# A six-stage transformer kernel on one core: the start of masked attention moved into the expert stage, and its scales by logarithm and exponential

## The chip, the cores and the metric

The kernel runs on one core of one Trainium2 chip. The metric is device microseconds of one execution, and the number compared is the median of several runs. Everything is fp32. The engines are TensorE (PE, with PEld for its weight loads), VectorE (DVE), ScalarE (ACT), GpSimd (POOL) and SyncE (SP, which here only issues transfers).

## What is computed

Six layers are applied to 64 batches of 32 rows of 128 numbers, each with a residual. The two that the change touches are the third, a soft mixture of 16 experts, and the fourth, masked cross attention over 257 keys for each batch:

```python
x = x + _L0_ffn_ref(_layernorm(x, axis=-1), ...)       # soft experts
x = x + _L1_xattn_ref(_layernorm(x, axis=-1), ctx_1024, mask_BxS2_bk0, ...)

def _L1_xattn_ref(query, key_value, key_mask, Wq, bq, Wk, bk, Wv, bv, Wo, bo):
    Q = query @ Wq + bq
    K = key_value @ Wk + bk
    V = key_value @ Wv + bv
    scores = jnp.einsum('bqh,bkh->bqk', Q, K) / jnp.sqrt(jnp.float32(hid))
    scores = jnp.where(key_mask[:, None, :], scores, jnp.float32(-1000000000.0))
    attn = jax.nn.softmax(scores, axis=-1)
    context = jnp.einsum('bqk,bkh->bqh', attn, V)
    return context @ Wo + bo
```

## The kernel before

The 2048 rows lie as 16 tiles of 128 rows in `xres`, four batches to a tile. The stages (cross attention, state space, experts, masked attention, causal attention, routed linear) run one after the other. Each is a block of five instruction streams, one for each engine, written out by hand, with semaphores between them. The next block begins on every engine only when all streams of the block before have ended; within a block an engine takes its instructions strictly in the order in which they are written.

**Experts, second part (`expert_layers`).** For each tile t, PE makes the slots' inputs (`gather`, L1828), ACT copies them out of PSUM (`slots_in`, L1880), PE makes the hidden layer (`hidden`, L1835), ACT applies Gelu (L1888), PE makes the second layer (`second`, L1848), DVE adds its bias (`slots_out`, L1907), PE mixes the slots back to rows (`combine`, L1858), and DVE adds the residual (L1912) and makes the row's mean and variance (L2905 to L2910, into `mv`). The PE's order is second(t), hidden(t+1), combine(t), gather(t+2). `gather(t)` waits for the Gelu of tile t-1, since both use a bank, and `second(t)` waits for the residual of tile t-1. GpSimd has no work in this block.

**Masked attention.** It goes in eight pairs of tiles. A pair's front is: rows normalised by DVE (`xn`, L2287), turned by PE (L2032), copied by ACT (L2182); queries by PE (L2037) and ACT (L2188); the queries times the keys' weights by PE (L2042, and a column of biases L2046) and ACT (L2194, `qk_t`), with the biases scaled by DVE (L2295, `qb`). Then the scores against the context (PE, L2056, `s_ps`), the mask (DVE, L2303 and L2311, with `keep` and `drop` made by GpSimd from the byte mask, L2389 and L2392), the exponentials (ACT, L2203), their transposes (PE, L2066, copied by DVE, L2325, `p_t`), the sums over the context (PE, L2089), and the values' and output's weights.

The fronts and scores of pairs 0 and 1 are made ahead; after that `slot(u)` finishes pair u and makes the front of pair u + 2. Before the fronts, the scales of all 16 tiles are made from `mv`: root of the variance on ACT (L83), reciprocal and product on DVE (L90, L92). GpSimd adds the output's bias to all of `xres` at once (L2408, `x_bo`), and DVE's slots wait for that. SP loads two context blocks of pair u + 2 (`room`): the first when pair u's scores are done, the second when its sums are.

Of the kernel before, what the change touches and what calls it, by code (L numbers as in the profile page):

```python
# [8 lines left out]
ALU = mybir.AluOpType  # L9
# [8 lines left out]
QT = 4  # L18
# [53 lines left out]
class NormScales:  # L72
# [1430 lines left out]
def soft_experts(nc, d, weights, xres, ident, mv, rstd, nmr):  # L1503

    C = 2
    with ExitStack() as outer:
# [5 lines left out]
        expert_layers(nc, weights[1], xres, mv, tok.x1, disp, comb_t)  # L1512
# [285 lines left out]
def expert_layers(nc, weights, xres, mv, xn, disp, comb_t):  # L1798
# [5 lines left out]
    with ExitStack() as stack:  # L1804
# [17 lines left out]
        def _(pe):  # L1822
# [29 lines left out]
            def combine(t):  # L1852
# [7 lines left out]
                last.then_inc(out_mm, 1)  # L1860
            pe.wait_ge(w_ld, W_LD)
# [1171 lines left out]
```

## Time and profile before

| | |
|---|---|
| median of three runs | 965.69 us (963.86, 965.69, 965.86) |
| the profiled execution | 960.14 us, of which the profile's span is 958.4 us |
| granted TensorE clock, mean over the span | 0.933 of full speed |
| busy over the span | PE 796.0, PEld 438.8, DVE 726.3, ACT 557.2, GpSimd 208.1 us |
| experts, second part | about 608.6 to 675.9 us |
| masked attention | about 676.9 to 759 us |

Times in the profile are microseconds from the start of its span. Busy shares are averages over six different stages, so they say little about one place; what matters for a change at a boundary of two stages is the order of events there, which the timeline shows. Matmul rows count passes: an fp32 matmul stands as two, a transpose as one.

### The profile page before, as it was taken

What the parts mean: (1) busy time and instruction counts of PE and PEld (TensorE: products, weight loads), DVE (VectorE), ACT (ScalarE), POOL (GpSimd) and SP (SyncE); (2) the same over time, 40 slices, a digit from 0 to 9 for tenths busy, and PEclk for the clock granted to TensorE, in tenths of its full rate; (3) what the DMA queues carried; (4) which work ended last, traced back from release to release, by engine and by line L of the source; (5) the groups of instructions that cost most, each with busy time, mean ns of one, the idle gap of its engine ahead of it and who ended that gap; (6) DMA issues with size and microseconds to landing.
All of it is one profiled execution on the core that took longest, in us unless ns stands there. A gap on an engine that the chain in (4) does not pass through costs nothing. (4 is left out here: it accounts for less than half of the span.)

```text
span 958.4 us, 25493 instructions
## 1 busy us (share of the span) xinstructions
PE 796.0 (83%) x9286; PEld 438.8 (46%) x9286; DVE 726.3 (76%) x2428; ACT 557.2 (58%) x1407; POOL 208.1 (22%) x228
## 2 busy tenths in 40 slices
PE   5899999998866689679757268799699999999876
PEld 2477777776422234224213056466376334343343
DVE  5688888887369999999999778465566486767866
ACT  3698988989674766757525147555244533333445
POOL 1366766766100000000000023000320000000046
PEclk9999999999997799889779599799699999999999
DMA  7111111110000000000000070300175000000001
GB/s 257 30 47 42 38 39 44 38 27 2 2 0 0 0 1 1 0 1 1 0 1 1 1 184 14 166 4 5 45 267 218 1 1 1 1 1 1 1 13 33
DMA packets 23422, 36.67 MB, mean 38 GB/s; under 512 B 5668, under 2 KB 19748, under 8 KB 21156
## 3 DMA queue, kind: packets, MB, share of 16 engines
q1 hardware_dynamic: 23336, 35.53, 11.8%
q8 instruction: 53, 0.87, 0.4%
q14 instruction: 33, 0.27, 0.1%
HBM read 34.48 MB, written 1.05 MB: 37 GB/s over the span
## 5 line engine op out<-in xcount | busy, mean ns | idle before, releaser
L505 ACT ACTIVATE xa_prob<-xa_s,xa_nmax 128x257 f32<-128x257 f32 x256 | 128.1, 503 | 21.1 <-DVE xa_nmax L642 19.3
L789 POOL TENSOR_TENSOR xa_prob<-xa_prob,xa_rinv 128x1028 f32<-128x1028 f32 x64 | 121.5, 1900 | 76.7 <-DVE xa_rinv L649 75.8
L642 DVE CUSTOM_DVE_ANT_0 xa_s<-xa_s_ps,xa_nbias 128x257 f32<-128x257 f32 x256 | 93.2, 420 | 12.3 <-ACT xa_prob L505 6.4
L1784 POOL TENSOR_TENSOR mo_disp_t<-mo_disp_t,mo_rst 128x256 f32<-128x256 f32 x16 | 9.8, 615 | 346.8 <-DVE mo_rst L1745 346.8
L335 PE MATMUL xa_t_ps<-identity,xa_prob 128*128 128x128 f32 x512 | 69.5, 279 | 4.0 <-ACT xa_p_t L514 1.8
L632 DVE COPY xa_kvs<-xa_kv_ps 128x512 f32<-128x512 f32 x64 | 44.1, 689 | 34.3 <-PE xa_kv_ps L309 34.3
L335 PEld LDWEIGHTS xa_t_ps<-identity,xa_prob 128*128 128x128 f32 x512 | 54.8, 141 | 25.6 <-issue 25.6
L514 ACT COPY xa_p_t<-xa_t_ps 128x1024 f32<-128x1024 f32 x64 | 63.4, 991 | 2.2 <-PE xa_t_ps L335 2.2
L948 PE MATMUL ss_bank<-ss_xs,ss_wx 128*128 128x512 f32 x128 | 58.9, 609 | 4.8 <-DVE ss_eps L1402 3.1
L2496 PE MATMUL ca_v_ps<-ca_w_vo,ca_xn_t 128*32 128x512 f32 x512 | 61.2, 596 | 0.5 <-DVE ca_v L2685 0.5
L962 PE MATMUL ss_bank<-ss_xs,ss_wx 128*128 128x512 f32 x128 | 59.9, 624 | 0.0
L2893 POOL TENSOR_TENSOR rl_part<-rl_part 128x256 f32<-128x256 f32 x16 | 11.9, 744 | 188.9 <-ACT rl_part L2841 188.3
L505 ACT ACTIVATION_READ_ACCUMULATOR xa_prob<-xa_s,xa_nmax 128x1 f32 x256 | 48.3, 189 | 0.0
L2489 PE MATMUL ca_z_ps<-ca_xn_t,ca_m_t 128*128 128x512 f32 x96 | 47.6, 618 | 0.7 <-ACT ca_xn_t L2606 0.7
L1131 ACT ACTIVATE ss_sq<-ss_bank 128x512 f32<-128x512 f32 x32 | 19.1, 597 | 49.4 <-PE ss_bank L962 49.4
L324 PE MATMUL xa_s_ps<-xa_kvs,xa_q_blk 32*128 32x257 f32 x512 | 46.2, 430 | 1.9 <-ACT xa_wv_last L485 1.2
L2685 DVE COPY ca_v<-ca_v_ps 128x512 f32<-128x512 f32 x64 | 41.4, 683 | 1.9 <-PE ca_v_ps L2496 1.9
L962 PEld LDWEIGHTS ss_bank<-ss_xs,ss_wx 128*128 128x128 f32 x128 | 25.2, 202 | 37.5 <-issue 37.5
L306 PE MATMUL xa_kv_ps<-xa_ctx_t,xa_wkv 128*32 128x256 f32 x512 | 40.5, 388 | 2.1 <-DMA xa_ctx_t<-in_ctx_t 2.1
L948 PEld LDWEIGHTS ss_bank<-ss_xs,ss_wx 128*128 128x128 f32 x128 | 24.1, 194 | 38.4 <-issue 33.0
L346 PE MATMUL xa_pv_ps<-xa_p_t,xa_kvs 128*32 128x128 f32 x1024 | 41.2, 279 | 0.0
L309 PE MATMUL xa_kv_ps<-xa_wkv,xa_ctx_t 128*32 128x128 f32 x1024 | 40.5, 277 | 0.0
(380 smaller groups left out, 1861.2 us busy)
## 6 DMA issues: line engine op xcount, KB each, us to landing
xa_ctx_t<-in_ctx_t SPq DMA_DIRECT2D x64, 128.5 KB, 2.1
room<-in_ctx_t SPq DMA_DIRECT2D x8, 1028.0 KB, 6.6
room<-in_ctx_n SPq DMA_DIRECT2D x8, 1024.0 KB, 4.9
ss_wx<-in_ss_wx SPq DMA_DIRECT2D x1, 2048.0 KB, 7.9
xres<-in_x SPq DMA_DIRECT2D x4, 256.0 KB, 5.5
out_x<-xres SPq DMA_DIRECT2D x4, 256.0 KB, 2.3
ma_mask_u<-in_mask SPq DMA_DIRECT2D x4, 128.5 KB
room<-in_ca_wk SPq DMA_DIRECT2D x1, 512.0 KB, 3.5
```

Source lines behind the costliest of these rows:

```text
L324: last = nc.tensor.matmul(s_ps[:, g, 0:S], q_blk[rows, r, :, :].rearrange("p h q -> p (h q)"), kvs[rows, r, 0:S], start=True, stop=True)
L335: last = nc.tensor.transpose(t_ps[:, c, g * P:g * P + P], prob[:, r, g, c * P:c * P + P], ident[:, :])
L505: nc.scalar.activation(prob[:, r, g, :], s_sb[:, b, g, :], ACT.Exp, bias=nmax[:, r, g:g + 1], scale=-1.0, accum_out=rsum[:, r, g:g + 1]).t ...
L514: nc.scalar.copy(p_t[:, b % 2, :, :], t_ps[:, :, :]).then_inc(pt_ready, 1)
L632: nc.vector.tensor_copy(kvs[:, r, :].rearrange("p (a s) -> p a s", a=2)[:, :, 0:SP_], kv_ps[:, :].rearrange("p (a s) -> p a s", a=2)).then ...
L642: nc.vector.tensor_tensor_reduce(out=s_sb[:, b, g, :], in0=s_ps[:, g, 0:S], in1=nbias[:, g, :], scale=1.0, scalar=3e38, op0=ALU.add, op1=A ...
L789: nc.gpsimd.tensor_tensor(prob[:, r, :, :], prob[:, r, :, :], bc(rinv[:, r, :].rearrange("p (g o) -> p g o", o=1), (P, G, S)), ALU.mult).t ...
L948: last = nc.tensor.matmul(bank[(2 + i) % 3][:, :], w_x[:, kb, 0, r, h, :], xs[:, c % 3, kb, :], start=(kb == 0), stop=(kb == 1))
L962: last = nc.tensor.matmul(bank[(1 + i) % 3][:, :], w_x[:, kb, 1, r, h, :], xs[:, c % 3, kb, :], start=(kb == 0), stop=(kb == 1))
L2489: nc.tensor.matmul(z_ps[:, n % 2, :], m_t[:, h, :], xn_t[:, QT * q:QT * q + QT, :], start=True, stop=True).then_inc(z_mm, 1)
L2496: last = nc.tensor.matmul(v_ps[N * h:N * h + N, b % 2, :], xn_t[:, t, N * b:N * b + N], w_vo[:, h, :, :], start=True, stop=True)
L2685: nc.vector.tensor_copy(v[:, j, b, :, :].rearrange("p g c -> p (g c)"), v_ps[:, b % 2, :]).then_inc(v_ready, 1)
```

## The change

- The fronts of pairs 0 and 1 (normalised rows, transposes, queries, query keys, bias columns) are made in the experts' block, for tiles 0 to 3, whose residuals have long been final there. DVE's part of normalising goes to GpSimd (`normalise`), DVE's scaling of the bias column to ACT.
- For the scales of tiles 0 to 3, ACT takes a logarithm and an exponential at tile 11, with a load of their table before and of Gelu's after. At the block's end it loads the first table again.
- GpSimd makes the masks of pairs 0 and 1 at the start of the experts' block, and `x_bo` tile by tile, after each residual.
- Masked attention begins with the scores of pairs 0 and 1. Its scales for all tiles are made by logarithm and exponential on ACT (the table is already there); only the product with the mean is left to DVE, after the first pair's masks.
- The tiles for `x_bo`, `keep` and `drop` lie in memory of the causal stage (`ca_xn_t`, `ca_z_first`), and `xn`, `xn_t`, `q_t` and `qk_t` are held twice.

```diff
-        self.root, self.eps = k.sb(f"{st}_norm_root", [P, T]), k.sb(f"{st}_norm_eps", [P, 1])
-        self.eps_set, self.root_ready, self.ready = (k.sem(f"{st}_norm_{n}") for n in ("eps_set", "root_ready", "ready"))
+    def __init__(self, k, st, mv, rstd, nmr, eps):
+        self.nc, self.mv, self.rstd, self.nmr, self.eps = k.nc, mv, rstd, nmr, eps
+        self.log_var = k.sb(f"{st}_norm_log", [P, T])
+        self.log_ready, self.ready = (k.sem(f"{st}_norm_{n}") for n in ("log_ready", "ready"))
 
     def scalar(self, act):
-        act.wait_ge(self.eps_set, 1)
-        self.nc.scalar.activation(self.root[:, :], self.mv[:, :, 1], ACT.Sqrt, bias=self.eps[:, :]).then_inc(self.root_ready, 1)
+        self.nc.scalar.activation(self.log_var[:, :], self.mv[:, :, 1], ACT.Ln, bias=self.eps[:, :]).then_inc(self.log_ready, 1)
+        act.wait_ge(self.log_ready, 1)
+        self.nc.scalar.activation(self.rstd[:, :], self.log_var[:, :], ACT.Exp, scale=-0.5).then_inc(self.ready, 1)
...
+        self.x_bo = sources.xn_t[:, :, :]
+        self.keep, self.drop = (masks[:, n * 4 * S:n * 4 * S + 4 * S].rearrange("p (j i s) -> p j i s", j=2, i=2) for n in range(2))
+        self.xn, self.xn_t, self.q_t = (k.sb("ma_" + n, [P, 2, 2, D]) for n in ("xn", "xn_t", "q_t"))
+        self.qk_t, self.qb = k.sb("ma_qk_t", [P, 2, 2, D]), k.sb("ma_qb", [P, 2, 2])
...
+def masks_of_pair(nc, pool, pairs, mask_u8, u, j, past):
+
+    nc.gpsimd.tensor_copy(pairs.keep[:, j, :, :], mask_u8[:, bass.ds(u * 2, 2), :]).then_inc(pairs.keep_ready, 1)
+    pool.wait_ge(pairs.keep_ready, u + 1)
+    pool.sem_inc(past, 1)
+    nc.gpsimd.tensor_scalar(pairs.drop[:, j, :, :], pairs.keep[:, j, :, :], -1e9, 1e9, ALU.mult, ALU.add).then_inc(pairs.drop_ready, 1)
...
+            def turn_x(u):
+                pe.wait_ge(pairs.xn_ready, u + 1)
+                for i in range(2):
+                    last = nc.tensor.transpose(turn_ps[u][:, i * P:i * P + P], pairs.xn[:, u, i, :], ident[:, :])
+                last.then_inc(pairs.xnt_mm, 1)
+
+            def queries(u):
+                if u == 0:
+                    pe.wait_ge(masked[1], masked[2])
+                pe.wait_ge(pairs.xnt_ready, u + 1)
+                nc.tensor.matmul(q_ps[u], w_q[:, :], pairs.xn_t[:, u, :, :].rearrange("p i c -> p (i c)"), start=True, stop=True).then_inc(pairs.q_mm, 1)
+
+            def query_keys(u):
+                pe.wait_ge(pairs.q_ready, u + 1)
+                nc.tensor.matmul(qk_ps[u], w_kt[:, :], pairs.q_t[:, u, :, :].rearrange("p i c -> p (i c)"), start=True, stop=True)
+                for i in range(2):
+                    last = nc.tensor.matmul(b_ps[u][:, i:i + 1], pairs.q_t[:, u, i, :], b_k[:, :], start=True, stop=True)
+                last.then_inc(pairs.qk_mm, 1)
             pe.wait_ge(w_ld, W_LD)
             gather(0)
             hidden(0)
             gather(1)
             for t in range(T):
                 second(t)
+                if t == T - 1:
+                    queries(1)
+                    query_keys(0)
                 if t + 1 < T:
                     hidden(t + 1)
+                if t == T - 2:
+                    turn_x(0)
+                    turn_x(1)
                 combine(t)
                 if t + 2 < T:
                     gather(t + 2)
+                if t == T - 2:
+                    queries(0)
+            query_keys(1)
...
+            def first_scales():
+                act.wait_ge(pairs.eps_set, 1)
+                act.wait_ge(pairs.mv_ready, QT)
+                nc.scalar.activation(pairs.log_var[:, :], mv[:, 0:QT, 1], ACT.Ln, bias=pairs.eps[:, :]).then_inc(pairs.log_ready, 1)
+                act.wait_ge(pairs.log_ready, 1)
+                nc.scalar.activation(rstd[:, 0:QT], pairs.log_var[:, :], ACT.Exp, scale=-0.5).then_inc(pairs.rstd_ready, 1)
+
+            def xnt(u):
+                act.wait_ge(pairs.xnt_mm, u + 1)
+                nc.scalar.copy(pairs.xn_t[:, u, :, :].rearrange("p i c -> p (i c)"), turn_ps[u]).then_inc(pairs.xnt_ready, 1)
+
+            def queries(u):
+                act.wait_ge(pairs.q_mm, u + 1)
+                nc.scalar.activation(pairs.q_t[:, u, :, :].rearrange("p i c -> p (i c)"), q_ps[u], ACT.Identity, bias=b_q[:, :]).then_inc(pairs.q_ready, 1)
+
+            def query_keys(u):
+                act.wait_ge(pairs.qk_mm, u + 1)
+                nc.scalar.activation(pairs.qk_t[:, u, :, :].rearrange("p i c -> p (i c)"), qk_ps[u], ACT.Identity, scale=NORM).then_inc(pairs.qk_ready, 1)
+                nc.scalar.activation(pairs.qb[:, u, :], b_ps[u], ACT.Identity, scale=NORM).then_inc(pairs.qb_ready, 1)
             nc.scalar.preload_act_table(ACT.Gelu)
             act.wait_ge(w_ld, W_LD)
             slots_in(0)
             hidden(0)
             for t in range(1, T):
+                if t == FIRST - 1:
+                    nc.scalar.preload_act_table_set("natural_log_exp_and_others")
                 slots_in(t)
+                if t == FIRST - 1:
+                    first_scales()
+                    nc.scalar.preload_act_table(ACT.Gelu)
                 hidden(t)
-            nc.scalar.preload_act_table(ACT.Sqrt)
+            xnt(0)
+            xnt(1)
+            nc.scalar.preload_act_table_set("natural_log_exp_and_others")
+            queries(0)
+            queries(1)
+            query_keys(0)
+            query_keys(1)
...
+        @block.gpsimd
+        def _(pool):
+            def normalise(u):
+                if u == 0:
+                    pool.wait_ge(pairs.rstd_ready, 1)
+                for i in range(2):
+                    t = 2 * u + i
+                    last = nc.gpsimd.tensor_scalar(pairs.xn[:, u, i, :], xres[:, t, :], mv[:, t, 0:1], rstd[:, t:t + 1], ALU.subtract, ALU.mult)
+                last.then_inc(pairs.xn_ready, 1)
+            pool.wait_ge(masked[1], masked[2])
+            for u in range(2):
+                masks_of_pair(nc, pool, pairs, mask_u8, u, u, past_p)
+            for t in range(T):
+                if t == FIRST - 1:
+                    normalise(0)
+                if t == FIRST:
+                    normalise(1)
+                pool.wait_ge(res_ready, t + 1)
+                nc.gpsimd.tensor_tensor(pairs.x_bo[:, t, :], xres[:, t, :], b_o[:, :], ALU.add).then_inc(pairs.xbo_ready, 1)
...
             for u in range(2):
-                turn_x(u)
-                queries(u)
-                query_keys(u)
                 scores(u, u)
...
             norm.scalar(act)
-            nc.scalar.preload_act_table_set("natural_log_exp_and_others")
             act.wait_ge(w_ld, W_LD)
-            xnt(0)
-            queries(0)
-            query_keys(0)
-            xnt(1)
-            queries(1)
             exps(0, 0)
-            query_keys(1)
             xnt(2)
             exps(1, 1)
...
+            nc.vector.memset(first.eps[:, :], EPS).then_inc(eps_set, 1)
+            scores(0, 0)
             norm.vector(dve)
-            nc.vector.memset(first.eps[:, :], EPS).then_inc(eps_set, 1)
-            normalise(0)
-            normalise(1)
-            scores(0, 0)
             normalise(2)
             scores(1, 1)
-            dve.wait_ge(xbo_ready, 1)
+            dve.wait_ge(xbo_ready, T)
             steps(dve, slot, 4)
             moments_of(U - 2)
...
-            masks_of(0, 0)
-            masks_of(1, 1)
-            nc.gpsimd.tensor_tensor(x_bo[:, :, :], xres[:, :, :], bc(b_o[:, :].unsqueeze(1), (P, T, D)), ALU.add).then_inc(xbo_ready, 1)
             steps(pool, slot)
```

PE's instructions from the experts' hidden layer of the last tile into the start of masked attention, before (`me_` are the experts' tiles, `ma_` masked attention's, `room` the context; the branches are the ends and beginnings of blocks):

```order
L1835 MATMUL me_in_ps<-me_slot_in,me_w 32x64 x16
L1858 MATMUL me_so_ps<-me_slot_out,mo_comb_t 64x128 x8
L1848 MATMUL me_so_ps<-me_w,me_hid 32x128 x32
L1858 MATMUL me_so_ps<-me_slot_out,mo_comb_t 64x128 x8
L1804 UNCONDITIONAL_BRANCH
L2025 UNCONDITIONAL_BRANCH
L2032 MATMUL ma_f_ps<-identity,ma_xn 128x128 x2
L2037 MATMUL ma_f_ps<-ma_xn_t,ma_w_q 128x256
L2042 MATMUL ma_f_ps<-ma_q_t,ma_w_kt 128x256
L2046 MATMUL ma_b_ps<-ma_b_k,ma_q_t 128x1 x2
L2056 MATMUL ma_s_ps<-room,ma_qk_t 32x257 x8
L2032 MATMUL ma_f_ps<-identity,ma_xn 128x128 x2
```

and of the change, up to the end of the experts' block:

```order
L1863 MATMUL me_in_ps<-me_slot_in,me_w 32x64 x16
L1893 MATMUL me_in_ps<-identity,ma_xn 128x128 x4
L1886 MATMUL me_so_ps<-me_slot_out,mo_comb_t 64x128 x8
L1900 MATMUL me_in_ps<-ma_xn_t,ma_w_q 128x256
L1876 MATMUL me_so_ps<-me_w,me_hid 32x128 x32
L1900 MATMUL me_in_ps<-ma_xn_t,ma_w_q 128x256
L1904 MATMUL me_in_ps<-ma_q_t,ma_w_kt 128x256
L1906 MATMUL me_in_ps<-ma_b_k,ma_q_t 128x1 x2
L1886 MATMUL me_so_ps<-me_slot_out,mo_comb_t 64x128 x8
L1904 MATMUL me_in_ps<-ma_q_t,ma_w_kt 128x256
L1906 MATMUL me_in_ps<-ma_b_k,ma_q_t 128x1 x2
```

Four transposes stand ahead of the next to last mixing, one query matmul ahead of the last second layer, and the other, with one pair's query keys, ahead of the last mixing; the last pair's query keys come behind it. Then masked attention's first rows on PE are:

```order
L2166 MATMUL ma_s_ps<-room,ma_qk_t 32x257 x16
L2142 MATMUL ma_f_ps<-identity,ma_xn 128x128 x2
L2176 MATMUL ma_p_ps<-identity,ma_prob 128x128 x4
L2187 MATMUL ma_l_ps<-identity,ma_p_last 4x128 x2
L2147 MATMUL ma_f_ps<-ma_xn_t,ma_w_q 128x256
L2199 MATMUL ma_c_ps<-room,ma_p_t 32x128 x16
```

The two pairs' scores follow each other (before, a front of four steps stood ahead of each), then the rows of pair 2 are turned.

ACT's instructions around tile 11 of the experts, before (Gelu of tile 10, copies and Gelu of tile 11, and so on):

```order
L1888 ACTIVATE me_hid<-me_in_ps,me_b 128x64 x4
L1880 COPY me_slot_in<-me_in_ps 128x512 x2
L1888 ACTIVATE me_hid<-me_in_ps,me_b 128x64 x4
L1880 COPY me_slot_in<-me_in_ps 128x512 x2
L1888 ACTIVATE me_hid<-me_in_ps,me_b 128x64 x4
```

and of the change:

```order
L1944 ACTIVATE me_hid<-me_in_ps,me_b 128x64 x4
L1972 ACT_TABLE_LOAD
L1936 COPY me_slot_in<-me_in_ps 128x512 x2
L1950 ACTIVATE ma_first_log<-mv,ma_eps 128x4
L1952 ACTIVATE rstd<-ma_first_log 128x4
L1976 ACT_TABLE_LOAD
L1944 ACTIVATE me_hid<-me_in_ps,me_b 128x64 x4
L1936 COPY me_slot_in<-me_in_ps 128x512 x2
```

One table load moved in between Gelu and the copies, and a logarithm, an exponential and another load between the copies and Gelu.

## Rows read from the trace of the kernel before

**Rows 1.** Timeline, experts' last tiles: start us, length us, engine, line, operation, [idle before <-releaser].

```profile
667.29 0.71 PE L1828 MATMUL me_in_ps<-mo_disp,mo_x 32*128 32x256 f32 x8
...
668.07 1.07 ACT L1880 COPY me_slot_in<-me_in_ps 128x512 f32<-128x512 f32 x2 [0.92 <-PE me_in_ps L1828]
...
669.79 1.25 PE L1858 MATMUL me_so_ps<-me_slot_out,mo_comb_t 128*64 128x128 f32 x16
...
669.91 0.93 ACT L1888 ACTIVATE me_hid<-me_in_ps,me_b 128x64 f32<-128x64 f32 x4 [0.77 <-PE me_in_ps L1835]
...
671.53 1.06 PE L1848 MATMUL me_so_ps<-me_w,me_hid 32*32 32x128 f32 x64 [0.48 <-DVE xres L1912]
...
673.37 1.25 PE L1858 MATMUL me_so_ps<-me_slot_out,mo_comb_t 128*64 128x128 f32 x16 [0.79 <-DVE me_slot_out L1907]
...
675.76 0.17 DVE L2910 COPY mv<-me_moments 128x2 f32<-128x2 f32 x1
```

**Rows 2.** Timeline, masked attention's first two pairs.

```profile
676.87 0.61 POOL L2389 CAST ma_keep<-ma_mask_u 128x514 f32<-128x514 uint8 x1 [69.74 <-POOLq L2920]
...
679.67 4.51 POOL L2408 TENSOR_TENSOR ma_x_bo<-xres,ma_b_o 128x2048 f32<-128x2048 f32 x1
...
679.80 4.71 DVE L2287 TENSOR_SCALAR ma_xn<-xres,rstd,nmr 128x128 f32<-128x128 f32 x2 [0.84 <-PE ma_f_ps L2032]
...
684.41 1.94 PE L2056 MATMUL ma_s_ps<-room,ma_qk_t 128*32 128x257 f32 x16 [0.47 <-ACT ma_qk_t L2194]
...
685.78 0.49 DVE L2303 SCALAR_TENSOR_TENSOR ma_s_keep<-ma_s_ps,ma_qb,ma_keep 128x257 f32<-128x257 f32 x1 [1.20 <-PE ma_s_ps L2056]
...
691.55 1.94 PE L2056 MATMUL ma_s_ps<-room,ma_qk_t 128*32 128x257 f32 x16 [0.47 <-ACT ma_qk_t L2194]
...
693.43 0.69 PE L2032 MATMUL ma_f_ps<-identity,ma_xn 128*128 128x128 f32 x2
...
696.18 1.28 PE L2089 MATMUL ma_c_ps<-room,ma_p_t 128*32 128x128 f32 x32
```

**Rows 3.** Windows: length, busy of PE, PEld, DVE, ACT, POOL, PEclk, DMA share, GB/s.

```profile
676.00:678.00 2.00, 0.00 (x0) 0.00 (x0) 0.63 (x5) 0.97 (x2) 0.93 (x2) 0.54 0.00 0
...
691.00:696.00 5.00, 4.53 (x27) 2.52 (x26) 2.58 (x9) 2.10 (x7) 0.91 (x3) 0.50 0.00 0
...
696.00:697.00 1.00, 1.00 (x25) 0.79 (x28) 0.00 (x0) 0.47 (x1) 0.80 (x2) 0.68 0.00 0
```

**Rows 4.** Timeline, ScalarE: a table load and the activation behind it (cross attention).

```profile
21.65 1.28 ACT L588 ACT_TABLE_LOAD   x1
...
22.95 0.51 ACT L505 ACTIVATE xa_prob<-xa_s,xa_nmax 128x257 f32<-128x257 f32 x1
```

**Rows 5.** Timeline, ScalarE: a logarithm of variances in masked attention.

```profile
735.91 0.28 ACT L2227 ACTIVATE ca_log_var<-mv,ca_norm_eps 128x4 f32<-128x4 f32 x1
```

**Rows 6.** Timeline, pairs further on in masked attention.

```profile
698.03 0.70 PE L2042 MATMUL ma_f_ps<-ma_q_t,ma_w_kt 128*128 128x256 f32 x2
...
698.55 0.59 DVE L2287 TENSOR_SCALAR ma_xn<-xres,rstd,nmr 128x128 f32<-128x128 f32 x2
...
698.56 0.50 PE L2046 MATMUL ma_b_ps<-ma_b_k,ma_q_t 128*128 128x1 f32 x4
...
699.54 1.07 PE L2056 MATMUL ma_s_ps<-room,ma_qk_t 128*32 128x257 f32 x16 [0.20 <-ACT ma_qk_t L2194]
...
700.48 0.88 DVE L2303 SCALAR_TENSOR_TENSOR ma_s_keep<-ma_s_ps,ma_qb,ma_keep 128x257 f32<-128x257 f32 x2 [1.22 <-PE ma_s_ps L2056]
...
701.30 0.60 PE L2066 MATMUL ma_p_ps<-identity,ma_prob 128*128 128x128 f32 x4
...
701.97 0.68 DVE L2325 COPY ma_p_t<-ma_p_ps 128x512 f32<-128x512 f32 x1
```

**Rows 7.** Groups of GpSimd's instructions: count | busy us, mean ns | idle before.

```profile
L2895 POOL TENSOR_TENSOR rl_part<-rl_part 128x128 f32<-128x128 f32 x16 | 7.3, 455 | 1.2
```

**Rows 8.** The page's DMA issues: KB each, us from issue to landing.

```profile
room<-in_ctx_t SPq DMA_DIRECT2D x8, 1028.0 KB, 6.6
```

More of the change, by code:

```diff
@@ L1795, in slots, with expert_layers @@
         slot(t, t % 2)
-def expert_layers(nc, weights, xres, mv, xn, disp, comb_t):
+def expert_layers(nc, weights, masked, pairs, xres, ident, mv, rstd, xn, disp, comb_t):
     SL, HID = 16, 32
@@ L1912, in residual @@
                 nc.vector.tensor_tensor(xres[:, t, :], xres[:, t, :], out_ps, ALU.add).then_inc(res_ready, 1)
-                statistics(nc, dve, t, xres, mv, stats, moments, res_ready, st_ready, mo_ready, past_v)
+                last = statistics(nc, dve, t, xres, mv, stats, moments, res_ready, st_ready, mo_ready, past_v)
+                if t < QT:
+                    last.then_inc(pairs.mv_ready, 1)
+            nc.vector.memset(pairs.eps[:, :], EPS).then_inc(pairs.eps_set, 1)
             dve.wait_ge(w_ld, W_LD)
@@ L1965, in masked_attention @@
         ctx_t, ctx_n, ctxt_in, ctxn_in = weights[1]
-        m_t, first = weights[2:]
-        x_bo = k.sb("ma_x_bo", [P, T, D])
-        keep, drop = k.sb("ma_keep", [P, 2, TP, S]), k.sb("ma_drop", [P, 2, TP, S])
-        xn, xn_t, q_t, qk_t = (k.sb("ma_" + n, [P, TP, D]) for n in ("xn", "xn_t", "q_t", "qk_t"))
-        qb, smin, rsum, rinv = (k.sb("ma_" + n, [P, 2, TP]) for n in ("qb", "smin", "rsum", "rinv"))
+        m_t, first, pairs = weights[2:]
+        x_bo, keep, drop = pairs.x_bo, pairs.keep, pairs.drop
+        xn, xn_t, q_t = (a[:, 0, :, :] for a in (pairs.xn, pairs.xn_t, pairs.q_t))
+        qk_t, qb = pairs.qk_t, pairs.qb
+        smin, rsum, rinv = (k.sb("ma_" + n, [P, 2, TP]) for n in ("smin", "rsum", "rinv"))
         s_keep, s_all = k.sb("ma_s_keep", [P, TP, S]), k.sb("ma_s_all", [P, 2, TP, S])
@@ L2385, in masks_of @@
             def masks_of(u, j):
-                if later(u, 1):
-                    pool.wait_ge(sall_ready, TP * (u - 1))
-                    pool.sem_inc(past_p, 1)
-                nc.gpsimd.tensor_copy(keep[:, j, :, :], mask_u8[:, bass.ds(u * TP, TP), :]).then_inc(keep_ready, 1)
-                pool.wait_ge(keep_ready, u + 1)
+                pool.wait_ge(sall_ready, TP * (u - 1))
                 pool.sem_inc(past_p, 1)
-                nc.gpsimd.tensor_scalar(drop[:, j, :, :], keep[:, j, :, :], -1e9, 1e9, ALU.mult, ALU.add).then_inc(drop_ready, 1)
+                masks_of_pair(nc, pool, pairs, mask_u8, u, j, past_p)
             def last_column(u, j):
@@ L2954, in program @@
         ctx = context_room(k, room)
-        run(soft_experts, (mo, me, joining, joined, ctx, tokens))
         sources = FirstSources(k)
-        run(masked_attention, (ma, ctx, joined[0], sources))
+        with ExitStack() as attention:
+            pairs = FirstPairs(Scope(nc, attention), sources)
+            run(soft_experts, (mo, me, joining, joined, ctx, tokens, ma, pairs))
+            run(masked_attention, (ma, ctx, joined[0], sources, pairs))
         routes = FirstRoutes(k, tokens.x1, tokens.mu_u)
```

50 lines of the change are left out of this document (29 added, 21 removed).

## The prediction

> **What bounds the kernel here.** The busy shares of the page say little about a boundary, so I read the timeline of the experts' last tiles first. There PE and ACT pass one tile around a ring. ACT sat idle for 0.92 us before its copies at 668.07, so Gelu had ended at 667.15; the next gather began on PE at 667.29, ACT's copies at 668.07, Gelu at 669.91 after another 0.77 us of waiting, and it ended at 670.84, which is 3.69 us after the Gelu before it [rows 1]. What ACT does in its two waits is free up to 0.92 and 0.77 us, and beyond that lengthens the ring. DVE's last instruction ends at 675.93 and masked attention's first starts at 676.87: 0.94 us from block to block [rows 1, 2].
>
> Then I read the timeline of masked attention's start. The reader is to see a serial stretch: scores of pair 0 at 684.41, of pair 1 at 691.55, pair 2's rows turned at 693.43, pair 0's sums over the context at 696.18 [rows 2]. From the block's first instruction to those sums it is 19.31 us. The long GpSimd addition (4.51 us) held up two normalisations of DVE (4.71 us), but these ended at 684.51, and PE would not have turned those rows before its scores were through at 686.35; that hold-up costs nothing today [rows 2]. Last, the windows: PE is idle at the boundary, its granted clock drops to the half (1.2 GHz, mean 0.54 in 676 to 678), stays at 0.50 through the two fronts and returns in the window 696 to 697 (mean 0.68, so at about 696.64), after PE had been busy without a break to speak of since 691.55 [rows 2, 3].
>
> **The sum, step by step.** It is made against the profiled execution (960.14 us; the three timed runs have their median 5.55 us above it).
>
> *Tile 11 on ACT.* A table load costs 1.30 us from its start to the next activation's [rows 4]. The first stands in the wait of 0.92 us: 0.38 beyond it. Behind the copies come a logarithm of 0.28 us and an exponential that waits for it, taken as long (I put both at 0.5 to 0.6), and the second load: 1.8 to 1.9 us in a wait of 0.77 [rows 1, 4, 5]: 1.05 beyond it. Everything goes around the ring, so **+1.4 us**. Bounds: +0.4 if only one of them shows, +1.8 if the short instructions take twice as long. On this price a page of the Trainium skill speaks against the change: "ScalarE: Activation LUTs", section "What ACT_TABLE_LOAD costs", gives 2.66 us for a switch, a drain of about 1.38 us being added to the 1.28 of the load. The trace disagrees: 22.95 less 21.65 is 1.30 [rows 4]. What a stall of that length would do stands among the rivals.
>
> *The experts' end.* Four transposes stand before combine(14): four take 0.60 us with the last one's latency [rows 6], I take 0.45. The first query matmul (0.53 from its start to the next one's, 698.03 to 698.56 [rows 6]) goes into the 0.48 us in which PE waited for the residual before second(15) [rows 1], so it is hidden; without that wait it would cost its 0.53. Second(15), 1.06 us, then ends near 673.04. Behind it come the other query matmul, 0.53, and one pair's query keys, 0.9 to 1.03 (698.03 to 699.06 [rows 6]). They fill the 0.79 us wait and more: combine(15) starts near 674.45 instead of 673.37 [rows 1], runs without the wait inside, and ends 0.85 later than before. ACT must have made the queries by 673.5: Gelu ends at 670.84, two copies of 256 columns are under 0.5 each (half of 1.07 is a copy of 512 [rows 1]), the load 1.30, an activation under 0.5: at 673.5 or 673.7, about even. The last query keys on PE (to 676.5) and ACT's two short activations (0.6) end the block near 677.1 instead of 675.93: **+1.2 us**, between 0.85 (DVE's end alone) and 2.0. Who waits for this is the whole next block.
>
> *Masked attention's start.* The fronts are gone; PE begins with the scores. DVE's first mask begins 0.94 us behind them at the full clock, 1.37 at the half [rows 2, 6]. Its four instructions take 1.49 us (700.48 to 701.97), a product 0.17 (as the small copy at 675.76), two normalised rows 0.59 [rows 1, 6]: pair 2's rows are ready at 3.2 us, or 3.7. From turning them to pair 0's sums was 2.75 us at the half clock [rows 2]; at the full clock DVE decides, with pair 1's masks 1.49 and the copy of the transposes 0.68 [rows 6]: sums at 5.6 us at the full clock, 6.5 at the half. ACT's logarithm and exponential of all tiles are done long before DVE asks. GpSimd makes pair 2's masks just then, beside DVE's minima of pair 1, which read two operands from SBUF; I add 0.2. I take 6.3 us for 19.31: **-13.0 us**, between -12.4 and -13.7.
>
> *The clock behind it.* PE is idle from about the last query keys to the first scores and half idle until pair 2's turn, so I expect the clock to fall again. Before, it came back 5.1 us after PE became steadily busy and 0.46 us into pair 0's sums [rows 2, 3]. If PE is steadily busy from 4 us after the block's start, it comes back at 9, that is 2.8 us into them. PE sets the pace there, and a microsecond at the half clock does 0.55 of one (1.07 against 1.94 us for the same scores [rows 2, 6]): 2.4 us more at the half clock cost **+1.0 us**, between 0 and 2.5.
>
> *Free.* GpSimd's sixteen additions, 0.455 us each [rows 7], begin behind the residual and end before DVE's small copy of the moments begins; masks at the block's start run while DVE has nothing. Were they not hidden, 7.3 us. The first context load is issued about 2 us after the block's start and lands 6.6 later [rows 8], at 8.6, and is needed 3.36 us after pair 0's sums (696.18 to 699.54 [rows 2, 6]), at 9.7. The later loads keep their distance to the sums. DVE's reciprocal and the root go, from a stretch already counted.
>
> Sum: 1.4 + 1.2 - 13.0 + 1.0 = **-9.4 us**: 950.7 for an execution like the profiled one, and a median of 965.7 - 9.4 = **956.3 us**.
>
> **Rivals.**
>
> *The clock.* Either it does not fall at all: then the start is 5.6 us, the clock term -0.2, the gain 11.3, time 954.4. For it: PE works to within 3 us of the new block's scores, before it was idle for 4.5 [rows 1, 2]. Or it stays at the half for longer, or falls already in tile 11's longer waits: 2 to 3 us more, gain near 7, 958.7. Chances 0.12 and 0.15.
>
> *Loads that stall ACT.* If each load were followed by a stall as long again (1.3 us), tile 11 would cost 2.6 us more and the end 1.3 us, since combine(15) stands behind queries that come late: gain 5.5, 960.2. Against it speaks the activation that follows at once [rows 4]. Chance 0.05. This is what the drain on the skill's page would do.
>
> *The start finds another wait.* Pair 2's context or pair 1's scores come late, since two pairs' scores share two banks and the second pair must wait for the first masks: the slots begin some 4 us later, gain 5.5, 960.2. The bank is free once a mask has read it, 1.4 us in, so it should not show. Chance 0.06.
>
> *GpSimd takes DVE's time in the experts.* In the trace two normalisations stood for the whole 4.51 us of an addition [rows 2]. If each tile's addition stopped DVE in the ring, one add a tile is 7.3 us: gain 2.1. It becomes slower from 0.71 us a tile on ((9.4 + 1.9) / 16); if DVE waits twice a tile, for 0.91 us, the time is 14.6 - 9.4 = 5.2 us longer, 970.9. What speaks against it is that only DVE's copy of the moments goes from SBUF to SBUF in the ring; the others read PSUM or one operand. The skill ("SBUF — State Buffer", "Who interferes with whom") says the same: an instruction with at most one SBUF input outside the two-port modes does not contend; rows 2 agree as far as a blocked normalisation goes. Chances 0.02 for one wait a tile or less, 0.03 for slower.
>
> *No effect,* if the slots have their pace from something that does not start earlier: 965.7. Chance 0.02.
>
> **How the numbers follow.** My forecast has 0.55, with 955 to 958. The range runs from no fall of the clock with the best bounds (about 12 us gained) to a late clock or one of the two waits (5 us): **953.4 to 960.6**. About 0.2%, 1.9 us, is what a measurement tells from no change. Faster has everything but the last cases: 0.94; same 0.03; slower 0.03.
>
> **What would show it.** On ACT, two gaps of 1.3 us at tile 11 and a ring there of 5.1 instead of 3.7 us. The experts' end 2.6 us later (about 678.5), with ACT's small activation as its last. The first scores on PE within 0.2 us of the block's start, pair 0's sums 6 to 6.5 us behind it, at 685.7 to 686.2 instead of 696.18. The granted clock at 0.50 through these. After that the same pace of pairs. I am wrong if the sums come on time and the pairs behind them are slower, if the ring is longer in every tile, or if the handover grows.

## The result, and the profile after

| | median | runs |
|---|---|---|
| before, beside it | 965.78 us | 963.86 to 966.51, 4 runs |
| changed | **954.76 us** | 956.0, 953.35, 955.04, 954.49 |

The ratio is 0.9884, 95% interval [0.9864, 0.9904]: 11.0 us less, where 9.4 were forecast. The two profiled executions differ by only 4.1 us (960.14 and 956.0), because the changed kernel's comes 5.5 us later to the experts' first gather (614.10 instead of 608.59), over code that is the same in both, and loses 0.8 us behind masked attention. So I compare stretches between fixed instructions. Block start is here the first row of masked attention on ACT (677.01 before, where GpSimd's first row was at 676.87 [rows 2]).

| stretch, us | before | changed | difference |
|---|---|---|---|
| experts' first gather to last gather | 58.70 | 60.23 | +1.53 |
| last gather to block start | 9.72 | 10.63 | +0.91 |
| block start to pair 0's sums over the context | 19.17 | 6.08 | -13.09 |
| these sums to the block's first `source` row on PE | 43.47 | 43.60 | +0.13 |
| all four | 131.06 | 120.54 | -10.52 |

The changed kernel's timeline at tile 11 (start us, length us, engine, line, operation, [idle before <-releaser]), against the ring of [rows 1]:

```profile
658.06 1.28 ACT L1972 ACT_TABLE_LOAD   x1
658.28 0.71 PE L1856 MATMUL me_in_ps<-mo_disp,mo_x 32*128 32x256 f32 x8
...
659.36 1.07 ACT L1936 COPY me_slot_in<-me_in_ps 128x512 f32<-128x512 f32 x2
...
660.32 0.31 ACT L1950 ACTIVATE ma_first_log<-mv,ma_eps 128x4 f32<-128x4 f32 x1
...
660.66 0.20 ACT L1952 ACTIVATE rstd<-ma_first_log 128x4 f32<-128x4 f32 x1
660.88 1.28 ACT L1976 ACT_TABLE_LOAD   x1
...
662.17 0.93 ACT L1944 ACTIVATE me_hid<-me_in_ps,me_b 128x64 f32<-128x64 f32 x4
...
663.25 0.50 PE L1856 MATMUL me_in_ps<-mo_disp,mo_x 32*128 32x256 f32 x4 [1.09 <-ACT me_hid L1944]
```

ACT has no idle bracket left in this tile: both waits are full. From gather to gather it takes 663.25 - 658.28 = 4.97 us, where the ring before it takes 3.78 and the three behind it 3.69. Both instructions of ACT that follow a load, a copy and a Gelu, begin 1.29 to 1.30 us after the load's start.

The end of the experts, same columns, against the last rows of [rows 1]:

```profile
677.40 1.09 PE L1886 MATMUL me_so_ps<-me_slot_out,mo_comb_t 128*64 128x128 f32 x16
...
678.42 0.70 PE L1900 MATMUL me_in_ps<-ma_xn_t,ma_w_q 128*128 128x256 f32 x2
678.43 1.28 ACT L1980 ACT_TABLE_LOAD   x1
...
679.05 1.07 PE L1876 MATMUL me_so_ps<-me_w,me_hid 32*32 32x128 f32 x64
...
681.45 1.09 PE L1886 MATMUL me_so_ps<-me_slot_out,mo_comb_t 128*64 128x128 f32 x16
...
683.68 0.17 DVE L3000 COPY mv<-me_moments 128x2 f32<-128x2 f32 x1
683.83 0.17 ACT L1965 ACTIVATE ma_qb<-me_in_ps 128x2 f32<-128x2 f32 x1
684.96 0.31 ACT L82 ACTIVATE ma_norm_log<-mv,ma_eps 128x16 f32<-128x16 f32 x1 [0.96 <-PEq L3010]
```

The last combine (681.45) runs without the wait inside that it had; DVE's last copy ends at 683.85 and ACT's bias column at 684.00: two ends 0.15 us apart. And masked attention's start, against [rows 2]:

```profile
685.13 3.54 PE L2166 MATMUL ma_s_ps<-room,ma_qk_t 128*32 128x257 f32 x32 [1.61 <-PEq L3010]
...
686.10 0.49 DVE L2402 SCALAR_TENSOR_TENSOR ma_s_keep<-ma_s_ps,ma_qb,ca_z_first 128x257 f32<-128x257 f32 x1 [1.03 <-PE ma_s_ps L2166]
...
688.11 0.60 DVE L2386 TENSOR_SCALAR ma_xn<-xres,rstd,nmr 128x128 f32<-128x128 f32 x2
...
688.77 0.53 PE L2142 MATMUL ma_f_ps<-identity,ma_xn 128*128 128x128 f32 x2
...
689.14 0.61 POOL L113 CAST ca_z_first<-ma_mask_u 128x514 f32<-128x514 uint8 x1
...
689.42 0.61 DVE L2410 CUSTOM_DVE_ANT_0 ma_s_all<-ma_s_keep,ca_z_first 128x257 f32<-128x257 f32 x1
...
690.31 0.68 DVE L2424 COPY ma_p_t<-ma_p_ps 128x512 f32<-128x512 f32 x1
...
691.04 0.53 PE L2199 MATMUL ma_c_ps<-room,ma_p_t 128*32 128x128 f32 x11 [0.58 <-DVE ma_p_t L2424]
```

Scores begin 0.17 us behind the block's start, and DVE works nearly without a pause from the first mask to the copy that the sums wait for. Last, the windows (length, busy of PE, PEld, DVE, ACT, POOL, PEclk, DMA share, GB/s), against [rows 3]:

```profile
685.00:686.00 1.00, 0.87 (x13) 0.56 (x16) 0.06 (x1) 0.48 (x2) 0.00 (x0) 0.80 0.00 0
686.00:688.00 2.00, 1.93 (x21) 0.60 (x16) 1.67 (x7) 0.26 (x1) 0.00 (x0) 0.50 0.22 33
688.00:689.00 1.00, 0.90 (x9) 0.23 (x2) 0.96 (x4) 0.84 (x4) 0.01 (x1) 0.50 0.67 181
689.00:690.00 1.00, 1.00 (x9) 0.88 (x9) 1.00 (x5) 0.37 (x1) 0.80 (x3) 0.99 1.03 436
```

TensorE's clock falls to the half at 685.6 (a mean of 0.80 is 0.6 us at full) and is back at 689.0, 2.0 us before pair 0's sums. Before, it came back 0.46 us into them.

### The profile page after: what moved, and what is told of

Its sections match the earlier page's. It is cut to its first block and busy times, and to the rows that moved or that the text cites. A ratio compares the mean times of both kernels' runs of the same rounds, so it can differ in the third digit from the quotient of the medians.

```text
span 954.2 us, 25511 instructions
## 1 busy us (share of the span) xinstructions
PE 800.3 (84%) x9286; PEld 441.4 (46%) x9286; DVE 720.1 (75%) x2421; ACT 559.7 (59%) x1413; POOL 214.5 (22%) x247
## 3 DMA queue, kind: packets, MB, share of 16 engines
HBM read 34.48 MB, written 1.05 MB: 37 GB/s over the span
```

## The experiments

Ten runs. For each the table gives the four stretches of its own profile; the text has times and ratios. Ratios are to the kernel before, run on the same chip.

| kernel | gathers | to block start | to pair 0's sums | to `source` | all |
|---|---|---|---|---|---|
| before | 58.70 | 9.72 | 19.17 | 43.47 | 131.06 |
| changed | 60.23 | 10.63 | 6.08 | 43.60 | 120.54 |
| changed_again | 60.10 | 10.63 | 5.93 | 44.73 | 121.39 |
| fronts_back | 59.57 | 9.59 | 18.62 | 43.82 | 131.60 |
| sum_at_once | 60.16 | 10.63 | 8.71 | 44.50 | 124.00 |
| behind_the_mixing | 59.65 | 11.55 | 6.36 | 43.37 | 120.93 |
| scales_by_newton | 58.33 | 10.62 | 5.73 | 43.92 | 118.60 |
| newton_again | 58.90 | 10.62 | 5.92 | 43.26 | 118.70 |
| loads_without_scales | 59.41 | 10.63 | 5.85 | 43.53 | 119.42 |
| second_layer_first | 58.33 | 11.37 | 5.98 | 44.17 | 119.85 |
| mixing_before_keys | 58.60 | 11.08 | 6.11 | 43.82 | 119.61 |
| additions_fivefold | 60.08 | 11.74 | 6.50 | 43.33 | 121.65 |

The column "to block start" is the steadiest: the six kernels that have the changed order at the experts' end and nothing added there show 10.62 or 10.63. The first column scatters by about half a microsecond. Two things stand out in it: six of the twelve profiles have a ring of 4.22 to 4.35 us at tile 7, in which PE stands still before the gather (0.60 us in the changed kernel, 0.49 in sum_at_once) and waits for nothing that the profile shows; and before and fronts_back have rings of 3.90 to 3.93 at tiles 11 to 13, where PE's second layer takes about 1.3 us instead of 1.07. The last column scatters by 1.5 us, and nearly all of that is PE's wait for a block of the context (`room`). Two such waits in the changed kernel, one in changed_again:

```profile
707.65 1.07 PE L2166 MATMUL ma_s_ps<-room,ma_qk_t 128*32 128x257 f32 x16 [0.28 <-DMA room<-in_ctx_t]
...
714.52 1.07 PE L2166 MATMUL ma_s_ps<-room,ma_qk_t 128*32 128x257 f32 x16 [0.18 <-DMA room<-in_ctx_t]
```

```profile
713.11 1.07 PE L2166 MATMUL ma_s_ps<-room,ma_qk_t 128*32 128x257 f32 x16 [1.67 <-DMA room<-in_ctx_t]
```

Before it is 0.31 us, in the other kernels 0.08 to 1.08. Without these waits the column is 43.06 to 43.16 in nine of the twelve, the kernel before and the changed one among them; sum_at_once (44.14), fronts_back (43.49) and additions_fivefold (43.25) stand out.

**fronts_back: is the gain in the fronts?** The rest of the change stays: `x_bo` tile by tile and the first masks in the experts, and masked attention's scales by logarithm and exponential.

```diff
 # experts: turn_x, queries, query_keys (PE, ACT), normalise (GpSimd), tile 11's loads and scales are left out
 # masked attention
             for u in range(2):
+                turn_x(u)
+                queries(u)
+                query_keys(u)
                 scores(u, u)
...
+            normalise(0)
+            normalise(1)
             scores(0, 0)
```

> Everything of the change stays (residual with bias and first masks in the experts, scales by logarithm and exponential) but the fronts of the first two pairs go back to masked attention's start, and tile 11 of the experts gets its two table loads back out. Theory (the chain of two cold fronts is the gain): the start is long again, key sums 18.3 to 19.5 us behind the block's first row, last gather to block start 9.6, the ring at tile 11 3.7; the time is 964.6 to 966.2, at most 0.8 under the kernel before. Rival (what blocked the start was VectorE standing behind GpSimd's 4.5 us sum): the key sums come 4 us earlier than before, and the time is 960 to 962.

964.83 us against 965.51 before (12 and 19 runs), ratio 0.9991 [0.9973, 1.0008]: the gain is gone. In its timeline the start is again the chain of cold fronts, though no long GpSimd addition stands beside DVE any more; its last window shows the clock's return:

```profile
682.39 0.31 ACT L82 ACTIVATE ma_norm_log<-mv,ma_eps 128x16 f32<-128x16 f32 x1 [4.73 <-PEq L2999]
...
683.93 0.66 PE L2118 MATMUL ma_f_ps<-identity,ma_xn 128*128 128x128 f32 x2 [3.81 <-DVE ma_xn L2373]
...
684.63 0.60 DVE L2373 TENSOR_SCALAR ma_xn<-xres,rstd,nmr 128x128 f32<-128x128 f32 x2 [0.84 <-PE ma_f_ps L2118]
...
701.01 1.25 PE L2175 MATMUL ma_c_ps<-room,ma_p_t 128*32 128x128 f32 x24
```

```profile
690.00:701.00 11.00, 9.50 (x48) 5.12 (x40) 4.75 (x17) 3.93 (x13) 1.84 (x5) 0.50 0.28 96
701.00:702.00 1.00, 1.00 (x25) 0.92 (x28) 0.00 (x0) 0.47 (x1) 0.80 (x2) 0.57 0.00 0
```

The second normalisation takes 0.60 us for both rows where it took 4.71 [rows 2], and the sums come 18.62 us behind the start all the same. So that hold-up cost nothing, as read, and the rival that it blocked the start falls. What else is in the change (scales by logarithm, sum and masks out of the way) is worth 0.55 us by the stretch, and nothing that the times tell.

**sum_at_once: does the sum have to leave the start?**

```diff
 # experts
-                nc.gpsimd.tensor_tensor(pairs.x_bo[:, t, :], xres[:, t, :], b_o[:, :], ALU.add)...
 # masked attention, GpSimd
+            nc.gpsimd.tensor_tensor(x_bo[:, :, :], xres[:, :, :], bc(b_o[:, :].unsqueeze(1), (P, T, D)), ALU.add)...
```

> The changed kernel with the residual plus bias as one GpSimd addition of 16 tiles at masked attention's start, behind its masks, as in the kernel before, in place of 16 in the experts. Theory (this part of the change is worth nothing by itself; it only has to be out of the way of the early sums): GpSimd's 4.5 us lie on top of VectorE's small operations at the start, whose stretched ones cost one operation's stretch of 0.2 to 4 us; key sums 6 to 10 us behind the block's first row, most likely 8; time 755 + 201 = 956 to 959. Rival (nobody waits there): 954.8 +-0.4, key sums at 6.1.

(In the expectation 755 is where the next stage begins in the changed kernel's profile, and 201 what follows.) 959.64 us, a little over the 956 to 959 expected; ratio 0.9942 [0.9916, 0.9968], an interval that lies above the changed kernel's. The timeline shows the place:

```profile
681.89 4.53 POOL L2497 TENSOR_TENSOR ca_xn_t<-xres,ma_b_o 128x2048 f32<-128x2048 f32 x1 [20.84 <-POOLq L3009]
...
684.01 2.69 DVE L2408 CUSTOM_DVE_ANT_0 ma_s_all<-ma_s_keep,ca_z_first 128x257 f32<-128x257 f32 x1
...
686.64 0.42 DVE L2408 CUSTOM_DVE_ANT_0 ma_s_all<-ma_s_keep,ca_z_first 128x257 f32<-128x257 f32 x1
```

DVE's minimum of pair 0, which reads two operands from SBUF, takes 2.69 us instead of 0.42 and ends just behind the addition (686.42). That is 2.27 of the 2.63 us by which the sums come later. The clock stays at the half for longer too (682.7 to 692.9), that is 2.3 us into pair 0's sums, and pair 1's sums come 7.39 us behind them (690.59 to 697.98) where they come 6.33 behind in the changed kernel (691.04 to 697.37). That is 1.06 us more, and it makes the last column 0.9 longer. Start and last column together are 3.5 us longer in this profile. The same addition was free before and costs here: with the fronts gone there is nothing left to hide it.

**additions_fivefold: do GpSimd's additions in the experts hold up DVE?**

```diff
                 nc.gpsimd.tensor_tensor(pairs.x_bo[:, t, :], xres[:, t, :], b_o[:, :], ALU.add)...
+                for n in range(4):
+                    nc.gpsimd.tensor_tensor(idle[:, n, :], xres[:, t, :], b_o[:, :], ALU.add)...
```

> The changed kernel with each of GpSimd's sixteen additions in the experts followed by four more of the same size into a scratch tile, 1.8 us more of GpSimd's work a tile. Theory (GpSimd's additions in the experts cost VectorE nothing): rings stay at 3.69 to 3.75, first to last gather 60.2 +-0.6, VectorE's operations as before (residual 0.29, slots 0.68 each). Rival (VectorE stands still while GpSimd works on the same memory): each of the four costs up to its 0.45 us when it lies over VectorE's, rings of 4.2 to 5.5, and 8 us or more over 16 tiles.

One run, 953.57 us. From tile 2 on the rings are 3.69 to 3.77 but for 4.98 at tile 11 and 4.22 at tile 7, and sum_at_once, which has no addition in the experts at all, has a ring of 4.25 there too; first to last gather takes 60.08 us. The groups by line of this kernel, and last the same group of the changed one (count | busy us, mean ns | idle before):

```profile
L2031 POOL TENSOR_TENSOR me_idle<-xres,ma_b_o 128x128 f32<-128x128 f32 x64 | 27.2, 458 | 0.0
L1999 DVE TENSOR_TENSOR xres<-xres,me_so_ps 128x128 f32<-128x128 f32 x13 | 3.7, 287 | 10.8 <-PE me_so_ps L1886 10.8
```

```profile
L1999 DVE TENSOR_TENSOR xres<-xres,me_so_ps 128x128 f32<-128x128 f32 x13 | 3.7, 288 | 10.8 <-PE me_so_ps L1886 10.8
```

27.2 us more of GpSimd leave DVE's residual at 287 ns. The ring pays nothing, and GpSimd's additions are as long as ever (458 ns). The block's end does pay: GpSimd's last addition ends at 682.81, later than ACT (681.75), and the next block starts 1.0 us behind it, 1.1 us late.

**scales_by_newton: what do tile 11's loads cost?** The four columns of scales come from GpSimd, with no table.

```diff
 # ACT, tile 11
-                    nc.scalar.preload_act_table_set("natural_log_exp_and_others")
-                    first_scales()
-                    nc.scalar.preload_act_table(ACT.Gelu)
 # GpSimd after tile 5; v = variance + EPS, y's bits = 0x5f3759df - v's bits / 2, then three times:
+                    a = y * y;  a = a * v;  a = a * -0.5 + 1.5;  y = y * a
```

> The changed kernel with the four columns of scales made on GpSimd after tile 5 by 14 small arithmetic operations (a starting value from the bits, three Newton steps) in place of ScalarE's logarithm and exponential at tile 11, so both table loads there fall away. Theory (the two loads and two activations are a wait of the whole ring at tile 11, worth 1.28 us in the profile): ring at tile 11 back to 3.7 us, time 953.2 to 953.8, 1.0 to 1.5 less than the changed kernel's. Rival (the ring would have waited there for something else, or GpSimd's small operations hold VectorE): ring over 4.4 and no measurable difference, 954.8.

951.13 us, ratio 0.9856 [0.9824, 0.9889], 2 us below the 953.2 to 953.8 expected. The ring at tile 11 is 3.70 us, as expected (4.99 and 5.03 in the two others of that chip that have the loads). GpSimd's chain, first and last row:

```profile
638.81 0.22 POOL L2017 TENSOR_SCALAR ma_first_log<-mv 128x4 f32<-128x4 f32 x1
...
642.49 0.20 POOL L2023 TENSOR_TENSOR rstd<-rstd,me_root_a 128x4 f32<-128x4 f32 x1
```

3.9 us of small operations, in time that GpSimd had idle. Here the clock did not fall at masked attention's start at all (1.00 in all windows from 682 to 688), and the start took 5.73 us. Whether that belongs to the shorter ring was asked of a second run.

**newton_again and changed_again, on one chip.** Both kernels unchanged, run once more.

> The changed kernel itself once more, to stand beside the one with GpSimd's scales on one chip: 954 to 956, 1.0 to 1.2% under the kernel before; in the profile ring at tile 11 of 4.97, last gather to block start 10.6, block start to key sums 6.1 with the clock halved for about 3 us.

> The kernel with GpSimd's scales once more, on the same chip as changed_again. Theory (1.28 us of ring gone, nothing else changed): 1.3 us below changed_again, with the clock halved at masked attention's start for about 3 us again, where its first profile showed no fall, and block start to key sums 6.1. Rival (the shorter ring also keeps the clock up, so 1.9 us as in the first profile): no fall in this profile either and 5.7 from block start to key sums.

952.95 us (ratio 0.9879 [0.9844, 0.9914]) and 952.43 us (0.9856 [0.9816, 0.9896]). The profiles agree with the theory: 60.10 and 58.90 us of gathers, ring at tile 11 of 4.96 and 3.70, and the clock of newton_again fell again. (The four stretches differ by more, 2.69 us, but 1.48 of that is the wait for the context, 1.67 us against 0.19.)

```profile
685.00:686.00 1.00, 0.68 (x12) 0.53 (x16) 1.00 (x5) 0.00 (x0) 0.00 (x0) 0.86 0.00 0
686.00:689.00 3.00, 2.90 (x20) 1.85 (x13) 2.92 (x12) 2.13 (x8) 1.54 (x3) 0.50 0.96 343
689.00:690.00 1.00, 1.00 (x23) 0.64 (x25) 0.45 (x2) 1.00 (x4) 0.62 (x3) 0.93 0.07 25
```

So the shorter ring by itself does not keep the clock up; what decided in the first profile stays open. By the profiles, 1.27 us is what the scales on ACT cost; by the times (0.5 us here, 3.6 between two chips) the difference of the two kernels is not resolved, so that 1.27 us stand on the profiles alone.

**loads_without_scales: loads or activations?** The same kernel with the two loads at tile 11 put back, without logarithm and exponential.

> The kernel with GpSimd's scales, with the two table loads put back on ScalarE at tile 11, but not the logarithm and the exponential (they are on GpSimd). Theory (ring grows by what ScalarE does beyond its slack of about 1.9 us a tile, in the order first load, copies, rest, Gelu): without 0.51 us of activations between the copies and the Gelu the ring is 4.4 to 4.5 us, against 3.70 without loads and 4.97 to 5.03 with everything; the first load stays hidden behind the wait for the gather. Rival (a load costs its whole 1.28 us wherever it stands): 3.70 + 2.56 = 6.3.

One run, 949.26 us, which is inside the spread of the kernels with GpSimd's scales. The ring is 4.53 us, 0.83 above 3.70:

```profile
651.74 1.28 ACT L1973 ACT_TABLE_LOAD   x1
653.03 1.07 ACT L1937 COPY me_slot_in<-me_in_ps 128x512 f32<-128x512 f32 x2
654.12 1.28 ACT L1976 ACT_TABLE_LOAD   x1
655.42 0.93 ACT L1945 ACTIVATE me_hid<-me_in_ps,me_b 128x64 f32<-128x64 f32 x4
```

Two loads, 2.6 us of ACT, lengthen the ring by 0.83: 1.30 in a wait of 0.92 and 1.30 in one of 0.77 leave 0.38 and 0.53, which is 0.91. My ring of 4.4 to 4.5 counted the first load as hidden and comes out 0.03 low; a whole load each would have been 6.3. The remaining 0.44 (to 4.97) are the two activations.

**behind_the_mixing, second_layer_first, mixing_before_keys: the order on PE at the end.** Order after hidden(15), turn_x and combine(14) ("s" second(15), "c" combine(15), "q" queries, "k" query keys of pair 0 or 1):

```diff
-q0 s q1 k0 c k1     # the changed kernel
+q0 s c q1 k0 k1     # behind_the_mixing
+s q0 q1 k0 c k1     # second_layer_first (scales on GpSimd)
+s q0 q1 c k0 k1     # mixing_before_keys (scales on GpSimd)
```

> The changed kernel, but the second pair's queries and the first pair's query keys are issued on TensorE behind the last tile's combine, not between its second layer and its combine. Theory (the end is a queue on TensorE: the inserted 0.59 + 0.50 us stand before the combine, whose rest is VectorE's residual and statistics and ends the block 1 us earlier if it isn't held; but ScalarE's copies of the fronts come last in both): last gather to block start 10.3 to 11.0 against 10.6, time 954.5 to 955.2, same. Rival (the combine held by them sets the end): 9.8 and 953.9.

> The kernel with GpSimd's scales (scales_by_newton), and on TensorE both pairs' queries behind the last tile's second layer, not the first's in front of it. Theory (the experts' end grew because TensorE stands at queries(0), which waits for ScalarE's copies, with second(15) ready behind it: there it began 1.05 us later than in the kernel before): second(15) about 1 us earlier, the end's last operations again ScalarE's of the second pair, last gather to block start 10.0 to 10.2 in place of 10.62; time 0.5 us less, 950.6 by the profile's own scale, which the run's times can't resolve. Rival (ScalarE's table load, not TensorE's order, sets the end): 10.5 to 10.7.

> As second_layer_first, and the first pair's query keys behind the last combine too. Theory: VectorE's tail of the last tile 1 us earlier, but ScalarE's last operation of the query keys at the same time, so last gather to block start 10.0 to 10.2, as in second_layer_first. Rival (VectorE's tail ends the block): 9.6, half a microsecond better than second_layer_first.

954.14, 954.40 and 952.98 us; ratios 0.9869 [0.9838, 0.99], 0.9885 [0.9856, 0.9914], 0.9885 [0.9862, 0.9907]. By their times none is told from the changed kernel. In the profiles all three ends are longer than 10.63: 11.55, 11.37, 11.08. Both theories on the end missed in all three. The row of second_layer_first:

```profile
675.23 1.09 PE L1887 MATMUL me_so_ps<-me_slot_out,mo_comb_t 128*64 128x128 f32 x16
...
676.37 0.29 DVE L1994 TENSOR_TENSOR xres<-xres,me_so_ps 128x128 f32<-128x128 f32 x1 [1.17 <-PE me_so_ps L1887]
...
676.81 1.06 PE L1877 MATMUL me_so_ps<-me_w,me_hid 32*32 32x128 f32 x64 [0.48 <-DVE xres L1994]
```

With nothing ahead of it, second(15) still waits 0.48 us for DVE's residual of tile 14, and begins 1.58 us behind the combine instead of 1.65. It had not been held by queries(0): they lay in this wait, as the prediction had put them, and I was wrong to expect a microsecond here. Taken out of it they stand behind second(15) (from 677.80 on), where PE has hardly a wait left to hide them, and ACT's last activation comes 7.35 us behind combine(14)'s start instead of 6.60. In behind_the_mixing DVE is ready earlier, but ACT's last activation comes 1.5 us behind DVE's last, and that is the end.

## Why the prediction was right, and where it was off

The main term, the cold start, came as forecast and for the reason given; of the four terms three were within a quarter of a microsecond, and the fourth, the clock, was not. The median, 954.76 us, lies just below the 955 to 958 of my forecast and next to 954.4, the time of the rival in which the clock does not fall. It did fall, so the median alone would point at the wrong mechanism.

*Tile 11 on ACT, +1.4: measured +1.28* (4.97 - 3.69), and 1.27 by taking it out. The mechanism (waits of 0.92 and 0.77 filled first) is what loads_without_scales shows. Logarithm and exponential took 0.56 us with the gap between them (660.32 to 660.88). The ring of the kernel before took 3.93 at this tile, one of its three long ones, so against that ring the cost is 1.04. Nothing followed the loads: the rival that they stall ACT for another 1.3 us falls. The Trainium skill, "ScalarE: Activation LUTs", section "What ACT_TABLE_LOAD costs", adds such a drain of about 1.38 us. The traces disagree: in all twelve profiles, wherever the instruction behind a load has no other wait, it begins 1.29 to 1.39 us after the load's start.

*The experts' end, +1.2: measured +1.05* from the last gather to the next block's first row, GpSimd's before and ACT's now (9.58 and 10.63), in the way described: query matmul in PE's wait, one pair's query keys in front of the combine, ACT's small activation last, and DVE's copy 0.15 us ahead of it. I had DVE's end 0.3 us ahead; the transposes in front of combine(14) cost 0.57 us (3.07 instead of 2.50 from the last gather), not 0.45, and part of it was given back by the combine's lost wait.

*Masked attention's start, -13.0: measured -13.23* (19.31 to 6.08). fronts_back shows that these are the fronts' microseconds. 0.2 us were put down for GpSimd's masks beside DVE's minimum of pair 1: the row has 0.61 instead of 0.42.

*The clock behind it, +1.0: this step failed.* It assumed that the clock would return 5.1 us after PE became steadily busy, hence 2.8 us into the sums. It returned 3.9 us after the first scores, and 2.0 before the sums, which is 4.8 us earlier in relation to them. The price of a microsecond at the half clock, 0.45 us, was right:

| | half clock after the start of pair 0's sums | pair 0's sums to pair 1's |
|---|---|---|
| before | 0.46 us | 6.53 us |
| fronts_back | 0.86 | 6.72 |
| sum_at_once | 2.31 | 7.39 |
| changed, and the eight others | none | 6.33 |

These are 0.20, 0.39 and 1.06 us more than 6.33, or 0.43 to 0.46 for each microsecond. So where +1.0 was forecast, the clock gave back 0.2 us. By the whole stretch from the sums to `source` (43.60 and 43.47 us) the term is +0.1: PE waited 0.46 us for blocks of the context, where it had waited 0.31, and without these waits the stretch is the same to 0.02 us, so small differences further on have taken the 0.2 back. That PE is steadily busy was no measure of when the clock comes back.

*The rival of another wait at the start* falls: the scores of both pairs run in one row of 3.54 us (in changed_again pair 1's wait 0.20 us for the first masks), and the first context block, issued 1.9 us behind the block's start, was not waited for. That the later loads keep their distance holds less well. The wait for the context lies further on, at the scores of pairs 4 and 5 (pair 6 before), and it is there with and without the change.

The sum with measured terms is 1.28 + 1.05 - 13.23 + 0.13 = -10.8, and 0.25 us more in the gathers makes it -10.5. Those 0.25 are a balance: the ring at tile 7 is 0.66 us longer and the one at tile 1 0.25, and the three long rings of before are gone, 0.7 us. Both kernels without the fronts in the experts have these three rings and none of the ten with them has, so they may belong to the change; no run tells. The sum agrees with the medians' -11.0. What was missed, 1.6 us of 11.0, is the clock term (0.9), the two costs (0.3) and the start (0.2); the rest isn't told from scatter.

*GpSimd in the experts, free: right*, with room to spare (additions_fivefold). *x_bo as one addition* was not in the sum, since the change takes it away; sum_at_once shows that having it out of the start is a part that the gain needs: 2.6 us in the start and 1.06 behind it in the profile, and 4.9 between the medians of two chips.

Not tried: the masks of the first pairs alone at masked attention's start with the fronts gone, and the scales by square root in the new order. fronts_back bounds all of the rest of the change only in the old order.

## What to carry to other kernels

A serial start at a boundary of two stages is worth moving even onto engines that look full: 2.3 us of costs in a ring and a queue bought 13 us. Price what is put into a full ring by what sticks out of each engine's wait there, and look at the order of the queue before moving anything out of a wait that hides it: the three orders tried at the end were all longer in their profiles. And when a start is shortened, go again through what was free behind it (an addition of 4.5 us here), because its cover may have been the thing removed.

## What the runs showed that I had not expected

The stretch at the half clock at masked attention's start did not vary with the work as I had assumed. It lasted 3.4 us in eight profiles, among them the changed kernel's (685.6 to 689.0) and newton_again's (685.7 to 689.1), though the fall came 0.5 us behind the first scores in the one, 2.0 in the other, and 0.5 ahead of them in additions_fivefold; 10.2 us in sum_at_once, where PE idled for 2.3 us before pair 2's rows (682.7 to 692.9); 20.5 in before and in fronts_back (681.4 to 701.9), whose starts are alternations of engines; and none in the profile of scales_by_newton. One execution of the same kernel may have the fall and another not, and the six times of scales_by_newton spread from 945.7 to 954.9 us with a mean clock from 0.943 to 0.927: a term below 2 us has to be read from stretches of the profile.
